# A layer's two batch norms: the low halves of their results computed by VectorE alone

## The reference, cut to what matters

```python
def _batchnorm(x, g, b):
    mu = jnp.mean(x, axis=0)
    var = jnp.mean(jnp.square(x - mu), axis=0)
    return (x - mu) * jax.lax.rsqrt(var + EPS) * g + b
...
for l in range(L):                      # L = 2
    ...
    attn = agg.reshape(n, D) @ Wo[l].T + bo[l]
    x = _batchnorm(x + attn, g1[l], beta1[l])
    ff = jax.nn.relu(x @ W1[l].T + b1[l]) @ W2[l].T + b2[l]
    x = _batchnorm(x + ff, g2[l], beta2[l])
```

## Time and profile before

| | |
|---|---|
| median of 3 runs | 1246.8 us (1242.3 to 1251.4) |
| profiled execution | 1250.26 us |
| its span, first to last instruction | 1248.4 us |
| mean clock granted to TensorE | 0.940 of full speed |
| PE busy | 1074.7 us (86%) |
| DVE busy | 785.0 us (63%) |
| ACT busy | 566.1 us (45%) |
| POOL busy | 436.9 us (35%) |

### The profile page before, as it was taken

One profiled execution on the slowest core, in us unless ns is written; L12 is line 12 of the kernel. 1 busy time (PEld: TensorE's weight loads), 2 busy tenths in 40 slices (PEclk: granted clock), 3 DMA queues, 4 the chain that ended last, 5 costly groups with the idle time before them and its releaser, 6 DMA issues. The chain is left out here.

```text
span 1248.4 us, 20276 instructions
## 1 busy us (share of the span) xinstructions
PE 1074.7 (86%) x6736; PEld 888.3 (71%) x6737; DVE 785.0 (63%) x2449; ACT 566.1 (45%) x1034; POOL 436.9 (35%) x482
## 2 busy tenths in 40 slices
PE   4778785999589999999899699859999999989933
PEld 2545453898578888888698699648888888879821
DVE  5665563232557777777577524247777777748878
ACT  5432331210356666666524320046666666643435
POOL 5655565000244444444212200124444444302314
PEclk9888897999889999999999899889999999999965
DMA  6010124734841212213200454563121211230153
GB/s 129 21 40 20 40 90 125 179 83 93 214 100 34 55 38 51 50 34 116 76 27 21 132 124 103 104 180 79 34 54 34 63 42 34 100 101 1 62 115 85
DMA packets 58472, 96.35 MB, mean 77 GB/s; under 512 B 15874, under 2 KB 39174, under 8 KB 58128
## 3 DMA queue, kind: packets, MB, share of 16 engines
q1 hardware_dynamic: 58348, 95.19, 30.9%
q10 hardware_dynamic: 36, 0.01, 0.0%
HBM read 37.55 MB, written 24.17 MB: 49 GB/s over the span
## 5 line engine op out<-in xcount | busy, mean ns | idle before, releaser
L786 POOL TENSOR_SCALAR probs<-probs,mass_inv 125x1250 f32<-125x1250 f32 x160 | 210.9, 1319 | 309.2 <-DVE mass_inv L909 309.2
L805 PE MATMUL banks<-k_stack,q_stack 128*125 128x416 f32 (+1 forms) x960 | 299.2, 398 | 12.4 <-DVEq L887 12.4
L870 ACT ACTIVATE probs<-probs,neg_peak 125x1250 f32<-125x1250 f32 x160 | 213.5, 1334 | 153.7 <-DVE neg_peak L923 153.7
L900 DVE CUSTOM_DVE_ANT_0 probs<-banks,scores_bias 125x416 f32<-125x416 f32 (+1 forms) x480 | 267.6, 583 | 24.6 <-PE banks L805 20.2
L819 PE MATMUL banks<-ident,probs 125*125 125x125 f32 x1600 | 260.4, 278 | 26.0 <-POOL probs L786 19.6
L819 PEld LDWEIGHTS banks<-ident,probs 125*125 125x125 f32 x1600 | 242.9, 189 | 49.1 <-POOL probs L786 23.2
L859 ACT ACTIVATE probs_t<-banks 125x500 f32<-125x500 f32 x320 | 152.6, 477 | 130.9 <-PE banks L819 130.8
L833 PE MATMUL banks<-probs_t,v_pair 125*64 125x250 f32 x1600 | 186.2, 379 | 0.9 <-ACT probs_t L859 0.9
L805 PEld LDWEIGHTS banks<-k_stack,q_stack 128*125 128x125 f32 x960 | 147.8, 192 | 40.4 <-issue 26.4
L891 DVE COPY probs_t<-banks 125x500 f32<-125x500 f32 x160 | 108.2, 676 | 74.0 <-PE banks L819 74.0
L475 PE MATMUL banks<-onehot_src,onehot_dst 125*125 125x512 bf16 x540 | 120.5, 387 | 32.9 <-POOL onehot_dst L290 17.5
(11 more groups left out here) (247 smaller groups left out, 1459.0 us busy)
## 6 DMA issues: line engine op xcount, KB each, us to landing
q_stack<-q_split SPq DMA_DIRECT2D x160, 125.0 KB, 2.4
scores_bias<-edge_bias SPq DMA_DIRECT2D x8, 1171.9 KB
edge_bias<-bias SPq DMA_DIRECT2D x10, 585.9 KB
k_stack<-k_hi SPq DMA_DIRECT2D x16, 312.5 KB, 4.6
k_stack<-k_lo SPq DMA_DIRECT2D x16, 312.5 KB, 5.6
resid<-residual SPq DMA_DIRECT2D x2, 2500.0 KB, 10.1
residual<-t SPq DMA_DIRECT2D x8, 625.0 KB, 2.9
values<-v_stage SPq DMA_DIRECT2D x2, 2400.0 KB
```

Of the source, the lines that this page charges most:

```text
L786: nc.gpsimd.tensor_scalar(probs[:, u % 4, :], probs[:, u % 4, :], mass_inv[:, u % 4:u % 4 + 1], 1.0, ALU.mult, ALU.mult).then_inc(att["pro ...
L805: mm = nc.tensor.matmul(pb[0:NT, t % 5, 0:sn], q_stack[:, n % 2, half, part, tile * NT:(tile + 1) * NT], k_stack[:, head * N + s0:head * N ...
L870: nc.scalar.activation(probs[:, u % 4, :], probs[:, u % 4, :], ACT.Exp, bias=neg_peak[:, u % 4:u % 4 + 1], accum_out=mass[:, u % 4:u % 4 + ...
L900: nc.vector.tensor_tensor_reduce(out=probs[:, slot % 4, s0:s0 + sn], in0=pb[0:NT, t % 5, 0:sn], in1=scores_bias[:, (n % GROUPS) * GROUP + ...
```

## The change

The six calls of `low` that GpSimd makes in each layer (three in each norm) go to VectorE, with the same operands and the same semaphores. In the first norm chunks 0 and 1 are done one behind the other after the moments of chunk 2, and chunk 2 before the last `summed` of chunk 3. In the second norm the low part of chunk c - 2 stands at the head of chunk c, and that of chunk 2 stands ahead of the last `normed`. GpSimd keeps its three pieces of `r_lo` and loses the wait for `h_lo` at its end.

```diff
                 @block.gpsimd
                 def _(pool):
 
-                    for c in range(DC - 1):
-                        low(pool, nc.gpsimd, c, t1, h1_hi, h1_lo, "h1_hi", "h1_lo")
                     for n in range(3):
                         pool.wait_ge(oph["done"], ojobs.index(("f", 1, n)) + 1)
                         rectified_low(nc.gpsimd, 1, n)
-                    for c in range(DC - 1):
-                        low(pool, nc.gpsimd, c, t2, h_hi, h_lo, "h_hi", "h_lo")
-                    pool.wait_ge(oph["h_lo"], DC - 1)
...
                         summed_moments(c, 0)
                         if c == 1:
                             normed(0, 0, t1, G1, BE1)
+                        if c == DC - 1:
+                            low(dve, nc.vector, c - 1, t1, h1_hi, h1_lo, "h1_hi", "h1_lo")
                         summed(c, 2)
                         summed_moments(c, 1)
                         summed_moments(c, 2)
...
                             normed(0, 1, t1, G1, BE1)
+                        if c == 2:
+                            for k in range(2):
+                                low(dve, nc.vector, k, t1, h1_hi, h1_lo, "h1_hi", "h1_lo")
                     normed(0, DC - 1, t1, G1, BE1)
                     low(dve, nc.vector, DC - 1, t1, h1_hi, h1_lo, "h1_hi", "h1_lo_last")
...
                             if c and n == 2:
                                 normed(1, c - 1, t2, G2, BE2)
+                            if c > 1 and n == 0:
+                                low(dve, nc.vector, c - 2, t2, h_hi, h_lo, "h_hi", "h_lo")
                             dve.wait_ge(oph["g_done"], 3 * c + n + 1)
                             chunk_moments(t2, c, n)
                         moments(c)
+                    low(dve, nc.vector, DC - 2, t2, h_hi, h_lo, "h_hi", "h_lo")
                     normed(1, DC - 1, t2, G2, BE2)
                     low(dve, nc.vector, DC - 1, t2, h_hi, h_lo, "h_hi", "h_lo_last")
```

## The result

The changed kernel takes 1262.17 us (median of 4 runs, 1261.64 to 1263.19), the kernel before 1247.78 us beside it: a ratio of 1.012, 95% interval 1.0081 to 1.0159. The profiled execution of the changed kernel took 1262.55 us, 1260.7 of it span. So it is slower by 1.2%, about what was forecast (0.93%, which lies inside the interval). The median is just on the other side of the line of 1%; the interval holds both sides of it.

What follows compares the result with a forecast made beforehand. VectorE's queue was taken to bound the first norm and a VectorE-ScalarE-VectorE chain the second. 2 x (4.33 + 1.47) = 11.6 us on the median of 1246.8 gave 1258.4 us, range 1252 to 1265.

Steps and rivals of the forecast that it cites:

- The first norm: VectorE, first norm: three low parts and a wait for chunk 2's high part add 4.33 us a layer, all on the path.
- The second norm: Second norm: low parts (4.11 us) and new waits for ScalarE (3.1), less 5.77 of ended stalls, add 1.47 us a layer.
- The sum: Both norms over two layers: 2 x (4.33 + 1.47) = 11.6 us, giving 1261.9 us profiled and 1258.4 us on the median.
- the forecast's own spread: Whole kernel: 3 to 4 us, mostly from scatter of runs and some from each wait, giving 1254.5 to 1262 us.
- the clock rival, Rival 2: TensorE's new pauses ahead of `f` and k = 3: the granted clock falls, 6 us more, 1264.4 us; chance 12%.
- Rival 1: VectorE, both norms: low parts find idle time and only the ended stalls count, 1243.5 us; chance 5%.
- Rival 4: VectorE, both norms: a low part costs less than `a_lo`, say 0.85 us instead of 1.37, 1252.2 us; chance 3%.
- the last `normed`: Sign, first norm on VectorE: it would come 4.3 us later, counted from the start of chunk 3's `summed`.
- Rival 3: Second norm: the stalls of the tiny instruction are not GpSimd's and stay, 7.2 us a layer, 1269.9 us; chance 3%.
- A fall at k = 3: TensorE, second pause: half of 5.9 us of work at the low clock, 3.0 us a layer, all on the path.
- The rule that two-operand work belongs on VectorE: Trainium skill's rule: two-input work is about twice slower on GpSimd (1.45 us against 2.87 here), so moving it promises a gain.

Runs made afterwards that it cites:

- experiment 8: Changed kernel plus one more same-size subtraction on VectorE in each first norm, ahead of the low parts of chunks 0 and 1: 1264.74 us, one run.
- experiment 2: Kernel before with only the second norm's low parts moved to VectorE, in the change's order; GpSimd keeps the first norm's: 1251.99 us, ratio 1.0021.
- experiment 6: The changed kernel run again unaltered, beside the kernel before: 1259.37 us (6 runs), ratio 1.0111.
- experiment 5: Changed kernel plus idle matmuls on TensorE, 24 ahead of `f` at k = 0 and 20 ahead of k = 3: 1260.51 us, ratio 1.0116.
- experiment 4: Kernel before with the stretched 128x1 instruction rewritten to have one operand in SBUF less; GpSimd keeps all low parts: 1248.3 us, ratio 0.9989.
- number 9: Kernel before; in the second norm GpSimd starts chunks 0 and 1 later, chunk 2's low part goes to VectorE behind the last `normed`: 1241.79 us, ratio 0.9941.
- number 1: Kernel before with only the first norm's low parts moved to VectorE; GpSimd keeps the second norm's: 1257.94 us, ratio 1.0076.
- number 7: Changed kernel plus one more same-size subtraction on VectorE in each second norm, ahead of chunk 0's low part: 1261.39 us, one run.
- number 3: Kernel before with the second norm's low parts on VectorE, each placed where its high part is already there: 1243.13 us, ratio 0.9963; repeated 1242.2 us, 0.9942.

## Why the prediction was right, point by point

**The first norm** was to cost 4.33 us a layer and cost 4.40. Its terms: two low parts 2.74 (measured 2.74), the wait for the high part of chunk 2 0.22 (0.33), one low part 1.37 (experiment 8: 1.38 to 1.40). `f` was to start at 656.15 and k = 3 at 669.62; less the 1.41 us of a later start they came at 656.19 and 669.69. That nothing hides the work is shown by experiment 8.

**The second norm** was to cost 1.47 and cost 1.5 (experiment 2). The waits were to be 2.03, 1.49 and about 0.3 and were 1.95, 1.40 and 0.35. The stalls were to go, and went.

**The sum** of 11.6 us compares with 5.93 + 5.91 = 11.8 us in the blocks where the clock stays full (experiment 6). The medians say 14.4 us (1262.17 - 1247.78) and, in experiment 6, 11.5 us (1259.37 - 1247.92), the intervals of their ratios reaching 5 and 3.6 us to either side; 11.8 us is 0.95% and lies in both. What the first median has above it is no more than that scatter can hold, and the blocks show only 0.59 us of it, the fall at k = 3. Part of the near hit of the first profile is luck: 1261.9 us was worked out for it and it took 1262.55, but a start 1.41 us later and 1.5 us less in the rest, neither of them in the sum, cancelled.

**The chances.** I gave "within 1%" 0.50 and "slower by over 1%" 0.47; the median lies just on the second side, and neither interval settles the side. With 11.6 against a bound of 12.5 us that is the toss it was called. The first median, 1262.17 us, is also at the edge of the forecast's own spread (1254.5 to 1262), and the range to 1265 had been drawn so as to hold the clock rival too; that the range held says little between the two, and it is experiments 5 and 6 that decide. Below, the range was said to reach half-way to rivals 1 and 4, but 1252 is rival 4's own 1252.2. In the mechanism of the two norms nothing was wrong. One sign was misput: the last `normed` was to come 4.3 us later against the start of chunk 3's `summed`, but that `summed` itself moves by 2.74; the 4.4 us are counted from the start of the norm.

**Rival 1** (cover) failed where it was said to decide: VectorE has 0.27 us free there and not 4. The one longer idle stretch of this norm, 1.27 us ahead of the reciprocal of chunk 0, lies where no high part exists yet. **Rival 3** is excluded by experiments 2, 4 and 9. **Rival 4** would need a low part of 0.85 and it takes 1.37 to 1.40.

**Rival 2** (the clock) was half right, and mis-sized. The prediction expected a clock of 1.00 in both pauses and named a fall as a sign that the forecast is wrong; the clock did fall, and the forecast stood because a fall is cheap here. In the four profiles of the changed kernel or of near versions whose pauses were not filled or lengthened (after, numbers 1, 6 and 7) it fell in 3 of 14 pauses of 2.8 to 2.9 us; two more pauses, each behind a fall at k = 0, were cut to 1.49 and 1.56 us and had none. In number 8, where the pause ahead of k = 0 is 4.20 us, it fell in both layers. The chance of 12% rested on one fall, 3.3 us behind the last work. The same trace has two others at the end of the blocks, some 5.1 us behind TensorE's last work there (697.08 to 702.2) and some 2.1 us (1184.84 to 1186.9), so that one figure could not say what 2.8 us would do.

A fall at k = 3 was priced at 3.0 us, half of 5.9 us of work at the low level, and costs 0.59. The loss of working time was about right (2.65 us at the first `g`). The error was to count it as if TensorE were on the path from there on; the three waits for `r_lo` take up all but 0.59 us of it. At k = 0 it was rightly put at nothing.

**The rule that two-operand work belongs on VectorE** was rightly set aside: 1.45 against 2.87 us for each, and 1.2% slower for all of them. Numbers 3 and 9 show both ways round it at once: with the same six operations of the second norm on VectorE, in another place, the kernel gains, and by the medians it gains as much with two of each three left on GpSimd at another time.

## What to carry to other kernels

Moving an operation to an engine that does it twice as fast does not pay by itself. In a queue that sets the end of a stage it costs its whole time, unless it falls into a gap or takes more away there than it brings (number 3: 5.77 us of stalls against 3.20 that the low parts cost there). Read the queue's idle time at the place of insertion, and count the wait that it brings and what is queued behind. If an instruction is stretched to end with another engine's, what helped here was to shift one of the two in time (number 9) or to take the other away (number 3); changing the form of the stretched one handed the stall to its successor. And compare stretches inside two traces before medians: they agreed to 0.02 us, but for the one fall of the clock, where runs scatter by 9.

## What the runs showed of the hardware

- A VectorE instruction on only 128x1, with two tensors in SBUF, waited out a subtraction on GpSimd: 2.51 us for 0.22. The reciprocal and the tensor-scalars of the same size did not (0.15 to 0.28 us beside it). `normed`, a tensor-scalar on 128x1250 float32, did: 2.85 us for 0.93, and done 0.66 us after GpSimd.
- GpSimd's own time does not suffer from it: 2.93 us with VectorE waiting, 2.91 us beside the statistics.
- In idle stretches of 2.8 to 2.9 us the clock granted to TensorE fell in some executions of one and the same code and not in others (two of three in one profile, none of four in the next), and it came back at 660.9 in the one case (work from 657.60 on) and between 1168 and 1170 in the other (work from 1163.59 on).
